# Self-attention: the products of a step in 12 blocks at single score places, and 11 key tiles in GpSimd's partial sum

## The reference, cut to what matters

```
qkv = h @ qkv_w + qkv_b                        # h: (2, 2048, 512)
q, k, v = split(qkv)                           # 16 heads of 32 channels
scores = einsum('bqhd,bkhd->bhqk', q, k) / sqrt(32)
attn = softmax(scores, axis=-1)                # over 2048 keys
out = einsum('bhqk,bkhd->bqhd', attn, v)
```

## Time and profile before

| | us |
|---|---|
| median of 3 runs | 4107.65 (4102.2 to 4109.66) |
| the profiled execution: time | 4100.01 |
| its span (first to last instruction) | 4098.2 |
| attention's steps within it | about 947.7 to 2752 |

### The profile page before, as it was taken

The page is one execution under the profiler, slowest core; times in us unless marked ns, Lnnn a source line. Parts: engine busy times, 40 slices in busy tenths (PEclk is TensorE's granted clock), DMA queues, the critical chain, the costliest instruction groups (busy, mean ns, idle before and its releaser), DMA issues. The chain is left out here.

```text
span 4098.2 us, 51860 instructions
## 1 busy us (share of the span) xinstructions
PE 3742.3 (91%) x19596; PEld 2429.3 (59%) x19596; DVE 2275.0 (56%) x3956; ACT 1874.2 (46%) x3431; POOL 2085.4 (51%) x955
## 2 busy tenths in 40 slices
PE   4799969979999999999999999976999949999998
PEld 2577748854444444444444444425777737888887
DVE  2466642237777777777777777714666625222222
ACT  1465631114666666666666666654556521111111
POOL 0356630005787777787777877765676543000000
PEclk8698879978999999999999999997999969999999
DMA  7566646752120312102131201114566651111110
GB/s 230 137 159 176 171 153 218 229 152 62 26 58 23 67 26 48 46 16 65 27 67 27 58 23 26 32 46 114 148 176 165 160 199 41 58 41 41 41 41 31
DMA packets 213511, 371.45 MB, mean 91 GB/s; under 512 B 36103, under 2 KB 52999, under 8 KB 209703
## 3 DMA queue, kind: packets, MB, share of 16 engines
q1 hardware_dynamic: 213287, 368.49, 32.9%
HBM read 215.54 MB, written 144.51 MB: 88 GB/s over the span
## 5 line engine op out<-in xcount | busy, mean ns | idle before, releaser
L1955 DVE TENSOR_REDUCE a_peak<-a_sm 128x1 f32<-128x512 f32 x2048 | 1275.8, 681 | 483.1 <-PE a_sm L1795 480.5
L1909 ACT ACTIVATE a_e<-a_st 128x512 f32<-128x512 f32 x2048 | 1083.7, 596 | 659.7 <-PE a_st L1817 658.2
L2020 POOL TENSOR_TENSOR a_esum<-a_esum,a_e 128x2048 f32<-128x2048 f32 x256 | 1172.2, 4579 | 123.1 <-ACT a_e L1909 101.7
L1817 PE MATMUL a_st<-a_q,a_k 128*128 128x512 f32 x2048 | 869.0, 427 | 6.9 <-ACT a_e L1909 4.5
L1795 PE MATMUL a_sm<-a_k,a_q 96*128 96x512 f32 x2048 | 827.7, 411 | 27.8 <-DMA a_k<-s_k 27.8
L1817 PEld LDWEIGHTS a_st<-a_q,a_k 128*128 128x128 f32 x2048 | 386.3, 189 | 523.3 <-ACT a_e L1909 280.8
L1830 PE MATMUL a_acc<-a_e,a_v 128*32 128x512 f32 x4096 | 545.7, 605 | 15.4 <-ACT a_sums L1923 14.4
L1795 PEld LDWEIGHTS a_sm<-a_k,a_q 96*128 96x128 f32 x2048 | 397.6, 194 | 117.1 <-issue 28.2
L2157 PE MATMUL mlp_ph<-mlp_us,mlp_w_hi 128*128 128x512 f32 x1024 | 337.1, 392 | 33.0 <-DVE mlp_raw_lo L2206 33.0
L2199 ACT ACTIVATE mlp_gelu<-mlp_ph,mlp_b 128x512 f32<-128x512 f32 x128 | 88.1, 688 | 595.1 <-PE mlp_ph L2157 595.0
L2214 DVE CAST mlp_gs<-mlp_gelu 128x512 fp32r<-128x512 f32 x128 | 92.7, 724 | 457.5 <-ACT mlp_gelu L2199 457.5
(11 more groups left out here) (150 smaller groups left out, 5093.3 us busy)
## 6 DMA issues: line engine op xcount, KB each, us to landing
p_qs<-s_q SPq DMA_DIRECT2D x192, 256.0 KB, 5.7
s_q<-p_qo SPq DMA_DIRECT2D x64, 512.0 KB, 7.3
a_q<-s_q SPq DMA_DIRECT2D x96, 256.0 KB, 4.9
a_k<-s_k SPq DMA_DIRECT2D x24, 1024.0 KB, 15.6
s_x<-p_x SPq DMA_DIRECT2D x16, 1024.0 KB, 4.3
s_u<-p_ut_hi SPq DMA_DIRECT2D x64, 256.0 KB, 5.8
s_u<-p_ut_lo SPq DMA_DIRECT2D x64, 256.0 KB, 6.4
p_us<-s_u SPq DMA_DIRECT2D x16, 1024.0 KB, 7.8
```

Source lines behind the costliest of these rows:

```text
L1817: pe.matmul(st[0:KR, place(kt, h) % RING], k[:, g % 2, h, kt * P:kt * P + KR], q[:, j % QR, h], start=True, stop=True).then_inc(score_done, 1)
L1909: act.activation(e[0:KR, (j * NKT + kt) % ER, h], st[0:KR, place(kt, h) % RING], ACT.Exp, scale=SCALE).then_inc(score_read, 1)
L1955: dve.tensor_reduce(dst, src, AX.X, ALU.max).then_inc(unit_read, 1)
L2020: pool.tensor_tensor(esum[:], e[:, slot(0)] if x == 1 else esum[:], e[:, slot(x)], ALU.add).then_inc(e_added, 1)
```

## The change

The places are set one by one instead of by rule. `POOLED` has eleven tiles (ten additions), `SUMMED` (added up by TensorE) five: 3, 5, 8, 10, 15. `products(i, j, x)` stands between score x and unit x, with 12 blocks:

| place | products | place | products |
|---|---|---|---|
| 4 | add_up 15, weigh 14 (of the step before) | 35 | weigh 6 |
| 9 | add_partial, weigh 15 (of the step before) | 40 | weigh 7 |
| 14 | weigh 0 | 45 | weigh 8 |
| 20 | weigh 1, 2, 3 | 50 | add_up 8, weigh 9 |
| 25 | add_up 3 | 55 | add_up 10, weigh 10, 11 |
| 30 | weigh 4, add_up 5, weigh 5 | 63 | weigh 12, 13 |

The peaks are turned after place 59 (before: 55), `fetch_sums` comes after exponential 9 (before: 3), `spread_inverse` after exponential 37 (before: 19), VectorE's three parts after units 16, 24 and 52. GpSimd keeps `lower_parts` ahead of its eighth addition, the one of tile 12 (the seventh is now that of tile 11 instead of tile 10), and does `scale` before its ninth of ten instead of its sixth of nine.

```diff
--- before.py
+++ after.py
@@ -1614,17 +1614,19 @@
     QR = 4
     ER = 4
 
-    POOLED = [t for t in range(NKT - 2) if t % 3 != 2] if NKT > 2 else []
+    POOLED = [0, 1, 2, 4, 6, 7, 9, 11, 12, 13, 14]
+    SUMMED = [3, 5, 8, 10, 15]
+    SUMMED_FIRST = [5, 10, 15]
     ADDS = max(len(POOLED) - 1, 0)
     STEPS = B * GROUPS * CHUNKS
     BODY = STEPS
-    TURN_KT = max(NKT - 3, 0)
-    TURN = GH * (TURN_KT + 1)
+    TURN = 60
     HEAD = 14 if NKT > 1 else U
     TILES = GH * NKT + 1
     RING = 3
     LATE = 1 if NKT > 1 else 2
-    DIVIDE_AT = (6, 8, 32) if NKT > 1 else range(4)
+    DIVIDE_AT = (16, 24, 52)
+    FETCH_AT, SPREAD_AT = 9, 37
     SETUP = 2 + KW % 2
     with nc.cleanup_on_exit(), ExitStack() as ctx:
         sb = lambda n, s, t=F32: ctx.enter_context(nc.sbuf_tensor(f"{name}_{n}", s, t))
@@ -1829,53 +1831,71 @@
                     rows = slice(h * DH, (h + 1) * DH)
                     mm = pe.matmul(acc[rows, 0], v[0:KR, g % 2, kt, rows], e[0:KR, (j * NKT + kt) % ER, h],
                                    start=(kt == 0), stop=(kt == NKT - 1), tile_position=(0, h * DH))
-                if kt in POOLED:
+                if kt in POOLED or kt in SUMMED_FIRST:
                     mm.then_inc(tile_used, 1)
 
             def add_up(i, j, kt):
 
-                if kt in POOLED:
-                    return
-                first = min(t for t in range(NKT) if t not in POOLED)
-                operands = [e[0:KR, (j * NKT + kt) % ER]]
-                if POOLED and kt == NKT - 1:
-                    pe.wait_ge(e_added, (BODY * i + j + 1) * ADDS)
-                    operands.append(esum)
-                for x, operand in enumerate(operands):
-                    for h in range(GH):
-                        mm = pe.matmul(acc[h * DH:(h + 1) * DH, 1], ones[0:KR], operand[:, h], start=(kt == first),
-                                       stop=(kt == NKT - 1 and x == len(operands) - 1), tile_position=(0, h * DH))
-                mm.then_inc(tile_used, 1)
+                pe.wait_ge(score_read, number(i, j, place(kt, GH - 1)) + 3)
+                for h in range(GH):
+                    mm = pe.matmul(acc[h * DH:(h + 1) * DH, 1], ones[0:KR], e[0:KR, (j * NKT + kt) % ER, h], start=(kt == SUMMED[0]),
+                                   stop=False, tile_position=(0, h * DH))
+                if kt not in SUMMED_FIRST:
+                    mm.then_inc(tile_used, 1)
+
+            def add_partial(i, j):
+
+                pe.wait_ge(e_added, (BODY * i + j + 1) * ADDS)
+                for h in range(GH):
+                    mm = pe.matmul(acc[h * DH:(h + 1) * DH, 1], ones[0:KR], esum[:, h], start=False, stop=True, tile_position=(0, h * DH))
+
+            def products(i, j, x):
+
+                if x == 4 and exists(i, j - 1):
+                    add_up(i, j - 1, 15)
+                    weigh(i, j - 1, 14)
+                elif x == 9 and exists(i, j - 1):
+                    add_partial(i, j - 1)
+                    weigh(i, j - 1, 15)
+                elif x == 14 and exists(i, j):
+                    weigh(i, j, 0)
+                elif x == 20 and exists(i, j):
+                    weigh(i, j, 1)
+                    weigh(i, j, 2)
+                    weigh(i, j, 3)
+                elif x == 25 and exists(i, j):
+                    add_up(i, j, 3)
+                elif x == 30 and exists(i, j):
+                    weigh(i, j, 4)
+                    add_up(i, j, 5)
+                    weigh(i, j, 5)
+                elif x == 35 and exists(i, j):
+                    weigh(i, j, 6)
+                elif x == 40 and exists(i, j):
+                    weigh(i, j, 7)
+                elif x == 45 and exists(i, j):
+                    weigh(i, j, 8)
+                elif x == 50 and exists(i, j):
+                    add_up(i, j, 8)
+                    weigh(i, j, 9)
+                elif x == 55 and exists(i, j):
+                    add_up(i, j, 10)
+                    weigh(i, j, 10)
+                    weigh(i, j, 11)
+                elif x == 63 and exists(i, j):
+                    weigh(i, j, 12)
+                    weigh(i, j, 13)
 
             def step(i, j):
-                turn = exists(i, j + 1)
                 units = units_of_step(i, j)
-                given, scores = 0, 0
-                if NKT == 1 and exists(i, j - 1):
-                    weigh_tiles(i, j - 1, [0])
-                for kt in range(NKT):
-                    for h in range(GH):
-                        if exists(i, j):
-                            score_tile(i, j, kt, h)
-                        scores += 1
-                        while given < len(units) and given * GH * NKT < scores * U:
-                            score_unit(i, *units[given])
-                            given += 1
-                        if NKT > 1 and h == 1:
-                            if kt == 0 and exists(i, j - 1):
-                                weigh_tiles(i, j - 1, [NKT - 1])
-                            if kt > 0 and exists(i, j):
-                                weigh_tiles(i, j, [kt - 1])
-                    if kt == TURN_KT and turn:
+                for x in range(GH * NKT):
+                    if exists(i, j):
+                        score_tile(i, j, x // GH, x % GH)
+                    products(i, j, x)
+                    if x < len(units):
+                        score_unit(i, *units[x])
+                    if x == TURN - 1 and exists(i, j + 1):
                         turn_peaks(i, j + 1)
-                for m, u in units[given:]:
-                    score_unit(i, m, u)
-
-            def weigh_tiles(i, j, tiles):
-
-                for kt in tiles:
-                    weigh(i, j, kt)
-                    add_up(i, j, kt)
 
             pe.sem_inc(tile_used, ER)
             pe.wait_ge(small_in, 2 * DMA)
@@ -1897,17 +1917,17 @@
                 act.wait_ge(score_done, turned(i, j) + 1)
                 act.activation(rows[3 * DH:P, j % 2], st[3 * DH:P, TURN % RING if j else 0], ACT.Copy).then_inc(score_read, 1)
 
-            def exponentials(i, j, kt):
+            def exponential(i, j, kt, h):
                 n = BODY * i + j
-                act.wait_ge(tile_used, n * NKT + kt + 1)
-                before = (kt - ER) % NKT
-                if before in POOLED and (kt >= ER or exists(i, j - 1)):
-
-                    act.wait_ge(e_added, (n - (kt < ER)) * ADDS + max(POOLED.index(before), 1))
-                for h in range(GH):
-                    act.wait_ge(score_done, number(i, j, place(kt, h)) + 1)
-                    act.activation(e[0:KR, (j * NKT + kt) % ER, h], st[0:KR, place(kt, h) % RING], ACT.Exp,
-                                   scale=SCALE).then_inc(score_read, 1)
+                if h == 0:
+                    act.wait_ge(tile_used, n * NKT + kt + 1)
+                    before = (kt - ER) % NKT
+                    if before in POOLED and (kt >= ER or exists(i, j - 1)):
+
+                        act.wait_ge(e_added, (n - (kt < ER)) * ADDS + max(POOLED.index(before), 1))
+                act.wait_ge(score_done, number(i, j, place(kt, h)) + 1)
+                act.activation(e[0:KR, (j * NKT + kt) % ER, h], st[0:KR, place(kt, h) % RING], ACT.Exp,
+                               scale=SCALE).then_inc(score_read, 1)
 
             def spread_inverse(i, j):
 
@@ -1923,16 +1943,14 @@
                 act.activation(sums[:, j % 2], acc[:], ACT.Copy).then_inc(acc_read, 1)
 
             def step(i, j):
-                if NKT == 1 and exists(i, j - 1):
-                    fetch_sums(i, j - 1)
-                for kt in range(NKT):
+                for x in range(GH * NKT):
                     if exists(i, j):
-                        exponentials(i, j, kt)
-                    if NKT > 1 and kt == 4 and exists(i, j - 1):
+                        exponential(i, j, x // GH, x % GH)
+                    if x == FETCH_AT and exists(i, j - 1):
+                        fetch_sums(i, j - 1)
+                    if x == SPREAD_AT and exists(i, j - 1):
                         spread_inverse(i, j - 1)
-                    if NKT > 1 and kt == 0 and exists(i, j - 1):
-                        fetch_sums(i, j - 1)
-                    if kt == TURN_KT and exists(i, j + 1):
+                    if x == TURN - 1 and exists(i, j + 1):
                         take_rows(i, j + 1)
 
             act.sem_inc(score_read, 2)
@@ -2033,18 +2051,12 @@
                 pool.tensor_tensor(o[:, j % 2], sums[:, j % 2, 0], inv_t[:, j % 2], ALU.mult).then_inc(scaled, 1)
 
             def step(i, j):
-                if POOLED and exists(i, j):
-                    for x in range(1, 6):
-                        add(i, j, x)
-                if exists(i, j - LATE):
-                    scale(i, j - LATE)
-                if POOLED and exists(i, j):
-                    for x in range(6, 8):
-                        add(i, j, x)
-                if exists(i, j + 1):
-                    lower_parts(i, j + 1)
```

(8 more changed lines are left out.)

## The result

The changed kernel takes 4041.61 us (median of 4 runs, 4039.68 to 4044.82), the kernel before 4108.65 beside it: ratio 0.9839, 95% interval 0.9822 to 0.9856, 67 us less. The forecast was 4027, 80 less, range 4008 to 4062.

A forecast was written before the change was run, and what follows sets the result against it. TensorE's queue bounds the step: 56.38 - 0.86 - 1.32 - 0.44 - 0.24 + 0.14 + 0.1 = 53.75 us; 30 x (-2.63) - 3.1 + 1.9 = -80, counted from the median 4107.65 to 4027, range 4008 to 4062.

The forecast's parts named there:

- Products and blocks: In TensorE's queue, one product fewer saves 0.86 us a step and four blocks fewer, at 0.33 each, save 1.32.
- The rival on the price: At TensorE's blocks: 0.33 us is paid for products' own waits, so fewer blocks bring nothing; 4068 us, chance 0.12.
- GpSimd: Its one extra addition, 4.65 us, costs nothing in a steady step; 0.9 us of cover at block 9.
- The rings of three: Scores and units between blocks: ScalarE's and VectorE's slower pace is covered, except +0.14 us at ScalarE's copy of the rows.
- the two stalls said to go: TensorE's waits for the sums at weigh of tile 0, 0.44 us, and at score 0, 0.24 us, both vanish.
- no stall up to k = 5: Unit k after a block starts at 0.1 + 0.47k, its bank free at -0.54 + 0.60k, so nothing waits.
- the third of the prediction's signs of being wrong: VectorE's 0.60 us pace showing as TensorE idle in the six- and eight-place gaps between blocks.
- 0.05 us to spare: After the sums' fetch, exponential 10 is 0.25 us late, yet score 13 gets its bank with this margin.
- ScalarE's copy of the rows: After exponential 59, this 0.6 us copy delays score 63: +0.14 us a step, bounds 0 and 0.6.
- The DMA's landing: The rows' DMA lands at 53.6 us, score 0 being due at 53.5: +0.1 a step, bounds 0 and 0.7.
- the smaller version of the second rival: Step's end, late rows' DMA and ring stall at places 62 or 63: +0.5 us a step, 4043; chance with full version 0.18.
- First and last: Step 0 saves 3.1 us net through fewer blocks; the last step, its end set by GpSimd, grows by 1.9.

The follow-up runs named there:

- a_pool10: The kernel after with tile 14 taken from GpSimd's sum and added up by TensorE at place 4 (23 products, nine additions): 4065.0 us, step 54.96.
- a_split: The kernel after with its block of three at place 20 split over places 17, 20 and 22 (14 blocks, same products): 4057.8 us, step 54.62.
- b_pool11: The kernel before with tile 8 also in GpSimd's partial sum (eleven tiles, ten additions), places otherwise unchanged: 4177.03 us, ratio 1.0156.
- a_peak448: The kernel after with VectorE taking its row peaks over 448 of each 512 keys: 4031.39 us (one run), step 53.80.
- a_turn56: The kernel after with the peaks turned after place 55 instead of 59: 4044.89 us, step 54.01.
- b_late0: The kernel before with weigh of tile 0 moved into tile 1's block and VectorE's first two division parts later: 4108.04 us, ratio 0.9994.
- a_tail: The kernel after with tiles 13 and 14 of the last step alone added up by TensorE: 4040.64 us, step 54.11.

## Why the prediction came out as it did

The mechanism was right: TensorE's queue sets the step, and products and blocks are its price. The working had 55.6 - 2.18 for them; the same sum over the measured steps is 55.5 and 53.3.

*Products and blocks*, -2.18: confirmed by a_pool10 (0.83 for 0.86) and a_split (0.3 for 0.33 a block). The rival on the price falls. The rule of the Trainium skill's page "TensorEngine Tiling (Array Packing)", section "Key Properties", that a change of the tiling mode drains the array, agrees with a price that goes with the block, 0.3 us here, and not with its products. That the price is a drain is not shown: the trace shows that the weight load has no lead at both edges of a block (1996.91 and 1997.91), and a unit without a lead loses 0.10 by itself (unit 19). No run tells the two apart.

*GpSimd*: covered as forecast. It waited for TensorE before each first addition (115 us in 31 steps), and TensorE never waited for it in a steady step; b_pool11 shows what happens without that cover.

*The failed term is "The rings of three"*, with the two stalls said to go. I had 0.24 a step left; measured is 0.70, +0.46.

The reason: I compared the time at which a bank is free with the start of the matmul. What waits is its weight load, 0.23 us earlier. Counted so, "no stall up to k = 5" becomes: no wait up to k = 3, a shortened lead at k = 4 (unit 24 and its like, 0.02 or less), a stall at k = 5 (unit 19, 0.10). Unit 54 is a k = 4, but VectorE's first peak behind its block starts 0.62 after the matmul instead of 0.54, and it pays 0.07. Units 18 and 59 add little; a_peak448 took 0.32 off with all four. This is the third of the prediction's signs of being wrong, in a small measure. The copy of the sums had "0.05 us to spare" by the same count and cost 0.09.

ScalarE's copy of the rows cost 0.2 behind place 59 and behind place 55 (a_turn56). That it is ScalarE's copy I read from the waits and from the stall that went along with it; no run took the copy away. The DMA's landing, said to coincide with the need, took 0.22 instead of 0.1 and once 1.7. ScalarE's copy of the rows and the DMA stayed within the bounds I gave, near twice the values I took; for VectorE's ring and for the copy of the sums I had given no bound, and there was one to give.

Over 30 steps: forecast -78.9, measured -65.9 (score 0 to score 0: 56.31 to 54.11), which is 0.43 a step missing. The base of 56.38, which was 56.31, has no part in it, for the saving was added up from its terms. Term by term: the stalls after were 0.46 more than forecast, and 0.06 more on the mean by the long step; the stalls before were 0.83 and not 0.68, so 0.15 more went; products, blocks and turn gave 2.12 instead of 2.18. The measured 4041.61 lies near the smaller version of the second rival (4043, the end of the step bunching up), but only 0.2 of the 0.46 came at the places that it names.

*First and last.* Step 0: -2.7 for -3.1. Last step to the next stage: +4.0 for +1.9. The chain of ten additions and `scale` was 47.9 us, as worked out; but it began 8.3 us into the step instead of 7.7, and after 5 us in which TensorE stood idle its last two products took 3.4 us instead of 1.9, at a granted clock of 0.57 on average in that window. The clock was no term of the sum.

*Profiled execution and median.* In attention's stage (score 0 of step 0 to the next stage) it is 64.6 us less; the rest is 4.2 more in these two profiles (0.9 ahead of the stage, 3.4 in the cross-attention behind it), 60.3 in all between the profiled executions, 67.0 between the medians. That I counted from a profiled execution 7.6 below its median cost nothing here, and could have.

## What to carry to other kernels

A ring's cover is counted to the weight load, not to the matmul: in this kernel the load stands 0.23 us ahead. Look at the weight loads' idle time, for a matmul of 0.47 instead of 0.40 looks punctual and isn't: a lead of 0.09 cost 0.02 or less, one of 0.03 or none 0.07 to 0.10. Fewer and larger groups of narrow products save their price at the edges (0.3 us a group here), until the gap between them is longer than the slower engine's lead in the ring. A copy that an engine does in the middle of its stream costs by what stands behind it: 0.6 us where the scores went on at their full rate (b_late0), 0.09 straight behind a block of two products, where ScalarE had caught up.

## What the runs showed that I had not expected

The granted clock fell at the end of the 5 us in which TensorE waited for GpSimd. The same windows as in the earlier trace rows, the last block of scores, the idle time and the two products:

```profile
2668.00:2675.00 7.00, 5.96 (x36) 2.19 (x40) 0.00 (x0) 4.24 (x8) 7.00 (x3) 1.00 0.11 39
2675.00:2680.60 5.60, 0.70 (x8) 0.00 (x0) 0.00 (x0) 0.00 (x0) 5.46 (x2) 0.97 0.00 0
2680.60:2684.10 3.50, 3.36 (x16) 0.59 (x16) 0.00 (x0) 0.00 (x0) 0.03 (x1) 0.57 0.00 0
```

0.57 is nearly the lower of the two levels (1.2 of 2.4 GHz). In a_tail, where TensorE did not wait there, the two products took 1.9 us.

And the rows' DMA, of the same size in each step, landed in 3.2 to 5.0 us when q's loads followed 1.2 us behind it (2027.09 and 2028.32), and in 3.2 to 3.4 in a_turn56, where they come later. That is not enough to blame the loads: the kernel before has one landing of 4.0 us, with the next load issued 6.1 us behind it (2292.50 and 2298.64). The medians differ by 0.07 us (3.29 after, 3.22 before). What makes the rare long landing is not shown.
